# Graph attention in a 16-sequence block: graph values by transfers, zero rows from token sums, label products on GpSimd

## What is computed

```python
row_zero = v.sum(-1) == 0
q_exp = where(row_zero[..., None], 0.0, q[:, None, :])
self_feat = concatenate([v, q_exp], -1) @ W_self.T + b_self
output = self_feat; kv = self_feat[:, :20]
for d in range(2):
    A = (adj if d == 0 else swapaxes(adj, 1, 2))[:, :, :20, :]   # int32, 11 labels an edge
    cond = A.sum(-1); vb = A @ w_bias + b_bias
    aff = where(cond > 0, q_d . k_d / 4, NEG) + vb                # 16 heads of 16 channels
    output += softmax(aff) @ kv, through Wout[d], + bout[d]
x = v + relu(output)
```

## Time and profile before

| | |
|---|---|
| three runs | 832.12, 834.24, 836.28 us, median 834.24 |
| profiled execution | 834.01 us, its span 832.3 us |
| busy share of the span | PE 92%, DVE 59%, ACT 57%, POOL 45% |
| share of weight loads (PEld) | 68% |
| graph stage | from 27.8 us to about 270 us |
| mean granted clock of TensorE | 0.981 of full speed |

### The profile page before, as it was taken

The page is one execution under the profiler, slowest core; times in us unless marked ns, Lnnn a source line. Parts: engine busy times, 40 slices in busy tenths (PEclk is TensorE's granted clock), DMA queues, the critical chain, the costliest instruction groups (busy, mean ns, idle before and its releaser), DMA issues.

```text
span 832.3 us, 15511 instructions
## 1 busy us (share of the span) xinstructions
PE 767.1 (92%) x4964; PEld 561.9 (68%) x4964; DVE 489.9 (59%) x1030; ACT 477.3 (57%) x765; POOL 370.9 (45%) x612
## 2 busy tenths in 40 slices
PE   4989999999998489999999999999878999999997
PEld 3878778788875245666665556666545888888885
DVE  1378888888888745666665566655433443444433
ACT  1334444444444357777777777777655655555553
POOL 0157575757573455555555555554730212222110
PEclk9989999999999889999999999999989999999999
DMA  8701312121300666556665666566600000000001
GB/s 248 246 23 48 95 48 91 49 92 49 93 14 13 116 115 115 116 115 115 114 115 112 109 110 117 108 116 113 115 14 1 1 26 26 26 25 14 26 26 39
DMA packets 68860, 65.58 MB, mean 79 GB/s; under 512 B 11089, under 2 KB 68049, under 8 KB 68817
## 3 DMA queue, kind: packets, MB, share of 16 engines
q1 hardware_dynamic: 67488, 64.87, 34.4%
q10 hardware_dynamic: 1328, 0.16, 0.1%
HBM read 48.09 MB, written 16.78 MB: 78 GB/s over the span
## 4 chain that ended last, share of the span: by engine, by line
PE 47%; ACT 8%; issue 5%; DVE 4%; DMA 1%; POOL 1%; SPq 1%; ACTq 0%; POOLq 0%
PE ps L1599 10%; PE ps L1613 10%; PE ps L1489 5%; PE ps L1475 5%; ACT probsT L828 4%; PE ps L1527 3%; PE ps L1427 3%; PE ps L1419 2%; PE ps L1508 2%; ACT w_ada L857 2%; PE ps L1442 1%; ACT projT L849 1%; DVE qk L1074 1%; DMA parts_dram<-w_ada 1%; PE ps L1411 1%
## 5 line engine op out<-in xcount | busy, mean ns | idle before, releaser
L828 ACT ACTIVATE probsT<-ps 128x1024 f32<-128x1024 f32 x128 | 130.8, 1022 | 48.6 <-PE ps L1475 46.6
L1222 DVE TENSOR_TENSOR hidden_low<-hidden,hidden_high 128x512 fp32r<-128x512 f32 x64 | 46.6, 728 | 107.7 <-ACT hidden_high L940 59.7
L1126 DVE TENSOR_REDUCE neg_max<-ps 128x4 bf16<-128x344 f32 x128 | 64.2, 512 | 58.2 <-PE ps L1442 57.3
L1475 PE MATMUL ps<-q_stack,k_stack 97*128 97x256 bf16 x512 | 79.7, 279 | 9.0 <-ACT probsT L828 6.0
L1475 PEld LDWEIGHTS ps<-q_stack,k_stack 97*128 97x128 bf16 x512 | 43.4, 99 | 65.9 <-issue 30.6
L937 ACT ACTIVATE hidden<-ps,b_fc 128x512 f32<-128x512 f32 x64 | 44.1, 690 | 69.7 <-PE ps L1599 69.7
L1489 PE MATMUL ps<-probsT,v_ones 128*32 128x256 f32 x1024 | 69.3, 389 | 9.6 <-ACT probsT L828 9.5
L617 POOL TENSOR_TENSOR scores<-scores,row_max 128x640 f32<-128x640 f32 x32 | 40.8, 1275 | 76.7 <-DVE row_max L975 76.7
L1419 PE MATMUL ps<-w_qkv,x1T 128*128 128x512 f32 x128 | 63.7, 621 | 2.8 <-DVE rest L1133 2.8
L1325 PE MATMUL ps<-x_res,w_q 128*128 (+1 forms) x256 | 63.1, 391 | 0.0
L1325 PEld LDWEIGHTS ps<-x_res,w_q 128*128 128x128 f32 x256 | 46.9, 193 | 10.9 <-issue 5.5
(11 more groups left out here) (177 smaller groups left out, 1882.9 us busy)
## 6 DMA issues: line engine op xcount, KB each, us to landing
parts_dram<-w_ada SPq DMA_DIRECT2D x96, 128.0 KB
q_stack<-parts_dram SPq DMA_DIRECT2D x96, 128.0 KB, 3.9
k_stack<-parts_dram SPq DMA_DIRECT2D x32, 256.0 KB, 6.4
adj<-in_adj SPq DMA_DIRECT2D x16, 440.0 KB, 4.2
xT<-in_xT SPq DMA_DIRECT2D x16, 256.0 KB, 2.9
x_in<-in_x SPq DMA_DIRECT2D x16, 256.0 KB, 2.7
k_stack<-parts_dram SPq DMA_DIRECT2D x32, 128.0 KB, 5.4
out_x<-result SPq DMA_DIRECT2D x16, 256.0 KB, 2.1
```

The source lines that it names most:

```text
L828: nc.scalar.activation(probsT[:, s % 4, :], ps[:, COLS:COLS + 2, :].rearrange("p a n -> p (a n)"), ACT.Exp).then_inc(exp_made, 1)
L1126: nc.vector.tensor_reduce(places[:, :, k], ps[:, ROW_BANKS[n % 2], 0:4 * KP].rearrange("p (a g) -> p a g", a=4), AX_X, ALU.max, negate=Tru ...
L1222: nc.vector.tensor_tensor(hidden_parts[1][:, s % H_SLOTS, :], hidden[:, s % RAW, :], hidden_parts[0][:, s % H_SLOTS, :], ALU.subtract).the ...
L1475: mm = nc.tensor.matmul(ps[:, COLS + j, kt * N:(kt + 1) * N], k_stack[:, par, place, kt * P:(kt + 1) * P], q_stack[:, par, place, :], star ...
```

## The change

- **Values by transfers.** In setup, PE makes the values with tokens on the partitions (three tiles of 120, 120 and 80 rows by 512 channels), ACT copies them, SP stores them to a DRAM tensor v_dram. In each turn four transfers bring the values of b into v_blocks, whose other elements are zero since the setup. The masks on POOL, the value transposes on PE and the copy on ACT are gone; k_all goes through four banks.
- **Zero rows from token sums.** SP loads x of batch f + 1 with tokens on the partitions into x_res, ACT copies it with an accumulated sum of each row (row_totals), DVE makes of these a diagonal of ones and zeros in bf16 (nonzero, in the turn before), and PE multiplies it by ones: cond is made from PSUM. The row sums on PE and nz are gone.
- **Label products.** ACT copies the edges to floats behind cond, POOL multiplies these in place by the label weights, behind the second subtraction; DVE keeps the counts.
- Waits follow: among them, the raw scores of b wait for cond of f, the output transposes of c for the output of c - 1.

```diff
+V_BATCHES = 6
+V_TILES = (B + V_BATCHES - 1) // V_BATCHES
...
+        v_dram = nc.dram_tensor("v_dram", (B * M, 2 * F), F32, kind="Internal").ap()
...
+                K_BANKS = (4, 0, 1, 2)
+
+                def v_count(v):
+                    return min(V_BATCHES, B - v * V_BATCHES) * M
...
+                    for v in range(V_TILES):
+                        sp.wait_ge(v_rows_out, v + 1)
+                        sp.dma_start(v_dram[v * V_BATCHES * M:v * V_BATCHES * M + v_count(v), :], v_rows[0:v_count(v), v, :]
+                                     ).then_inc(v_stored, 16)
...
+                    for v in range(V_TILES):
+                        act.wait_ge(v_rows_mm, v + 1)
+                        nc.scalar.activation(v_rows[0:v_count(v), v, :], ps[0:v_count(v), 5 + v, :], ACT.Copy).then_inc(v_rows_out, 1)
                     for c in range(2 * C2):
-                        act.wait_ge(kv_mm, 2 * c + 1)
-                        nc.scalar.activation(k_all[:, c, :], ps[:, 4, 0:B * M], ACT.Identity,
+                        act.wait_ge(kv_mm, c + 1)
+                        nc.scalar.activation(k_all[:, c, :], ps[:, K_BANKS[c], 0:B * M], ACT.Identity,
                                              bias=b_k[:, c // C2, c % C2:c % C2 + 1]).then_inc(kv_out, 1)
-                        act.wait_ge(kv_mm, 2 * c + 2)
-                        nc.scalar.activation(v_all[:, c, :], ps[:, 5, 0:B * M], ACT.Copy).then_inc(kv_out, 1)
...
+                    nc.vector.memset(v_blocks[:], 0.0).then_inc(v_zeroed, 1)
...
+                    for v in range(V_TILES):
+                        for k in range(C2):
+                            mm = nc.tensor.matmul(ps[0:v_count(v), 5 + v, :], feat20[:, k, v * V_BATCHES * M:v * V_BATCHES * M + v_count(v)],
+                                                  w_o[:, :, k, :], start=(k == 0), stop=(k == C2 - 1))
+                        mm.then_inc(v_rows_mm, 1)
                     for c in range(2 * C2):
                         d, f = c // C2, c % C2
-                        for bank, w in ((4, w_k), (5, w_o)):
-                            ge(pe, kv_out, 2 * c + bank - 5)
-                            for k in range(C2):
-                                mm = nc.tensor.matmul(ps[:, bank, 0:B * M], w[:, d, k, f * P:(f + 1) * P], feat20[:, k, :],
-                                                      start=(k == 0), stop=(k == C2 - 1))
-                            mm.then_inc(kv_mm, 1)
+                        for k in range(C2):
+                            mm = nc.tensor.matmul(ps[:, K_BANKS[c], 0:B * M], w_k[:, d, k, f * P:(f + 1) * P], feat20[:, k, :],
+                                                  start=(k == 0), stop=(k == C2 - 1))
+                        mm.then_inc(kv_mm, 1)
...
+        def value_blocks(b, par):
+
+            ge(sp, mix_mm, b - 1)
+            rows = v_dram[bass.ds(b * M, M), :].rearrange("m (g h d) -> m g h d", g=H // 2, d=HD)
+            for h in range(4):
+                sp.dma_start(v_blocks[h * M:(h + 1) * M, par, :, h * HD:(h + 1) * HD], rows[:, :, h, :]).then_inc(v_in[par], 16)
+
+        x_by_batch = t["x"].rearrange("(b t p) f -> b p t f", b=B, p=P)
+
+        def x_tokens(f, par):
+
+            sp.dma_start(x_res[:, bass.ds(f * T, T), :], x_by_batch[bass.ds(f, 1)].rearrange("b p t f -> p (b t) f")
+                         ).then_inc(x_tokens_in[par], 16)
+
         def graph_turn(f, b, c, par):
-
             if f is not None and not (isinstance(f, int) and f == 0):
                 ge(sp, feat_mm, f - 1)
                 sp.dma_start(xT[:, par], t["xT"][:, bass.ds(f * N, N)].rearrange("(k p) n -> p k n", p=P)).then_inc(xT_in[par], 16)
-                ge(sp, lab_w, f - 1)
+                ge(sp, edges_float, f - 1)
                 ge(sp, cnt_made, f - 1)
+                ge(sp, diag_made, f)
                 sp.dma_start(adj[:, par].rearrange("p (t e) -> p t e", t=T),
                              t["adj"][bass.ds(f * N, N), :].rearrange("(t p) e -> p t e", p=P)).then_inc(adj_in[par], 16)
+            if isinstance(f, int) and f == 0:
+                x_tokens(0, 0)
+            if following(f) is not None:
+                x_tokens(following(f), 1 - par)
             if b is not None:
                 ge(sp, x_made, b - 1)
                 sp.dma_start(x_in[:, 1 - par], t["x"][bass.ds(b * N, N), :].rearrange("(t p) f -> p t f", p=P)
                              ).then_inc(x_arrived[1 - par], 16)
+                if isinstance(b, int) and b == 0:
+                    sp.wait_ge(g["v_stored"], 16 * V_TILES)
+                    sp.wait_ge(g["v_zeroed"], 1)
+                value_blocks(b, 1 - par)
...
+        def label_products(f):
+            pool.wait_ge(edges_float, f + 1)
+            edges = weighted[:].rearrange("p (e l) -> p e l", l=L)
+            nc.gpsimd.tensor_tensor(edges, edges, w_label[:].unsqueeze(1).broadcast_to([P, E2, L]), ALU.mult).then_inc(lab_w, 1)
...
             if f is not None:
-
-                ge(pool, vt_mm, 2 * f)
-                for k in range(2 * C2):
-                    nc.gpsimd.tensor_tensor(v_masked[:, k], v_all[:, k, bass.ds(f * M, M)].unsqueeze(1).broadcast_to([P, HT, M]),
-                                            own, ALU.mult).then_inc(vm_made, 1)
+                label_products(f)
...
+        def float_edges(f, par):
+            act.wait_ge(adj_in[par], loads(f, par))
+            ge(act, lab_made, f)
+            nc.scalar.activation(weighted[:], adj[:, par], ACT.Copy).then_inc(edges_float, 1)
...
-        def take_values(b, par):
-            act.wait_ge(vt_mm, 2 * b + 2)
-            ge(act, mix_mm, b - 1)
-            nc.scalar.activation(v_blocks[:, par], ps[0:G4, 0, :].rearrange("p (c v) -> p c v", v=64),
-                                 ACT.Copy).then_inc(vb_made, 1)
+        def row_totals(n, par):
+            act.wait_ge(x_tokens_in[par], loads(n, par))
+            ge(act, diag_made, n)
+            for tt in range(T):
+                nc.scalar.activation(summed[:, tt, :], x_res[:, bass.ds(n * T + tt, 1), :].rearrange("p a f -> p (a f)"), ACT.Copy,
+                                     accum_out=row_total[:, tt:tt + 1]).then_inc(totals_made, 1)
 
         def graph_turn(f, b, c, par):
+            if isinstance(f, int) and f == 0:
+                row_totals(0, 0)
             if f is not None:
 
-                act.wait_ge(nz_made, f + 1)
+                act.wait_ge(nz_mm, f + 1)
                 ge(act, feat_out, f)
                 for k in range(C2):
-                    nc.scalar.activation(cond[:, k, :], nz[:], ACT.Identity, bias=b_self[:, k:k + 1],
+                    nc.scalar.activation(cond[:, k, :], halves(ps, 4)[:, 0, :], ACT.Identity, bias=b_self[:, k:k + 1],
                                          scale=q_cond[:, k, bass.ds(f, 1)]).then_inc(cond_made, 1)
+                float_edges(f, par)
             if c is not None:
                 take_weights(c, 0)
                 take_weights(c, 1)
+            if following(f) is not None:
+                row_totals(following(f), 1 - par)
             if f is not None:
                 take_queries(f, par, 0)
             if b is not None:
                 exponentials(b, 1 - par, 0)
-                take_values(b, 1 - par)
                 exponentials(b, 1 - par, 1)
...
         def nonzero(f):
-
-            dve.wait_ge(sums_mm, f + 1)
-            ge(dve, cond_made, C2 * f)
-            nc.vector.tensor_scalar(nz[:], halves(ps, 4)[:, 0, :], 0.0, None, ALU.not_equal).then_inc(nz_made, 1)
+            dve.wait_ge(totals_made, T * (f + 1))
+            ge(dve, nz_mm, f)
+            nc.vector.scalar_tensor_tensor(out=nz_diag[:], in0=row_total[:].unsqueeze(2).broadcast_to([P, T, P]), scalar=0.0,
+                                           in1=ident_b[:].unsqueeze(1).broadcast_to([P, T, P]), op0=ALU.not_equal, op1=ALU.mult
+                                           ).then_inc(diag_made, 1)
 
         def features(f):
             dve.wait_ge(feat_mm, f + 1)
             dve.wait_ge(cond_made, C2 * (f + 1))
             nc.vector.tensor_tensor(feat_at(f), halves(ps, 1), cond[:], ALU.add).then_inc(feat_out, 1)
 
-        def label_products(f, par):
-
+        def edge_counts(f, par):
             dve.wait_ge(adj_in[par], loads(f, par))
-            edges = adj[:, par].rearrange("p (e l) -> p e l", l=L)
-            nc.vector.tensor_reduce(count[:], edges, AX_X, ALU.add).then_inc(cnt_made, 1)
-            nc.vector.tensor_tensor(weighted[:].rearrange("p (e l) -> p e l", l=L), edges,
-                                    w_label[:].unsqueeze(1).broadcast_to([P, E2, L]), ALU.mult).then_inc(lab_w, 1)
+            nc.vector.tensor_reduce(count[:], adj[:, par].rearrange("p (e l) -> p e l", l=L), AX_X, ALU.add).then_inc(cnt_made, 1)
...
         def graph_turn(f, b, c, par):
+            if isinstance(f, int) and f == 0:
+                nonzero(0)
             if f is not None:
-                nonzero(f)
```

(49 more changed lines are left out.)

48 lines of the change are left out of this document (25 added, 23 removed).

## The result

The changed kernel takes 845.12 us (median of 4, 839.76 to 847.50) where the kernel before took 834.30 in the same comparison: ratio 1.0131, 95% interval [1.0097, 1.0164], slower. The forecast was 836.0 in 821 to 845. The profiled execution has a span of 845.4 us, 13.1 more than before's 832.3. It is the longest of the four: its mean granted clock is 0.966, that of the others is 0.972, 0.973 and, in the one of 839.76 us, 0.981, where the kernel before has 0.977 to 0.985 in all 63 executions that ran beside the experiments. The medians are 10.8 us apart, so the 13.1 taken apart here are a little more than the usual execution has. The two tables of windows, cut at the same events (start of the graph stage, start of the third turn, start of the last, its end at the last raw scores, first `rest` on DVE), say where.

What follows compares the result with a forecast made beforehand. It took a loop over PE, DVE and POOL, 13.76 us a turn, as the bound. Start +4.7, graph turns -0.5, layernorm turn -1.0, last turn -1.4 gave +1.8 on 834.2: 836 us, range 821 to 845.

Steps and rivals of the forecast that it cites:

- PE alone could turn in 12.0: Steady graph turn: PE's own work and wait shrink by 1.85 us, so PE alone could turn in 12.0 us.
- They alternate, and the one that waited goes first: DVE with two SBUF inputs and POOL: one stands still until the other's instruction ends, then the waiting one goes.
- The turn stays at 13.8: Graph stage: a loop over the engines sums to 13.76 us a turn, gaining 0.5 us in place of 22.
- Rivals B: Graph turn: no_edge (L999) does not wait for the normalising; turn 13.1 us, kernel 828 us; chance 0.18.
- C: Graph turn: DVE's diagonal does not collide with POOL at all; turn 12.4 us, kernel 819 us; chance 0.12.
- I take 1.68, as 640 is the nearest size: POOL's label product: 880 elements at 1.70 ns each take 1.68 us, bounds 1.07 and 2.5.
- rival D: POOL's label product exceeds 1.68 us, its rows being short; every 0.1 us costs 1.3 us in all; chance 0.20.
- +4.7: Start: longer setup and late tokens put the first queries at 37.8 for 33.08 us; bounds +2.5 and +6.5.
- the 4.4 from there to the queries stay: Start: from the features' start at 33.4 us to the first queries at 37.8 remains 4.4 us.
- Behind it, DVE orders the transition as now: Transition behind the last graph turn: DVE sets its order as before, so no time was added.
- ACT "hidden": ACT's added copy and sums run hidden; if not, 0.9 us before the weight copies returns as PE's wait.
- A: The loop over the engines as counted, kernel 836 us, give or take 4; chance 0.50.

Runs made afterwards that it cites:

- number 5: Changed kernel with label products back on DVE, DVE diagonal moved ahead of the second scores, and tokens of batches 0 and 1 loaded in setup: 811.65 us.
- number 6: Changed kernel with POOL's label product cut from one instruction of 880 elements into two of 440: 832.05 us.
- number 12: Changed kernel with 8 products that nobody reads put on PE ahead of the first nonzero rows: 837.54 us.
- numbers 2: Changed kernel with the tokens of batches 0 and 1 loaded in setup, ahead of the late weights: 838.01 us.
- number 3: Changed kernel with the DVE diagonal moved ahead of the second scores and tokens of batches 0 and 1 loaded in setup: 820.49 us.
- number 1: Changed kernel with the DVE diagonal moved behind the edge counts, ahead of the second scores: 828.55 us.
- numbers 9: Changed kernel with 16 products that nobody reads put on PE ahead of the first nonzero rows: 841.58 us.
- number 8: Kernel before with only the label products moved: float copy on ACT, product on POOL behind the second shift: 867.19 us.

## Why the prediction was wrong, point by point

- **"PE alone could turn in 12.0":** right; number 5 turns in 12.06. (1.85 less in 13 turns is 24 us; the 25 is a slip.)
- **"They alternate, and the one that waited goes first":** right, and it carries the case. The diagonal ends 0.27 behind the label product (0.29 forecast), `no_edge` behind the normalising; number 6 shows that whole instructions exclude each other. That is the rule cited from the Trainium skill (SBUF — State Buffer, "Who interferes with whom"), and the trace agrees, with 1325 against 415 ns. By the page's rule alone one would not know who goes next; the rows say that.
- **"The turn stays at 13.8":** right in kind. The loop was counted as 13.76; with the label product at 1.92 in place of 1.68 it is 14.0, and eleven turns took 13.95. Rivals B (13.1) and C (12.4) are out.
- **"I take 1.68, as 640 is the nearest size":** wrong, mis-sized by 0.24 in each turn. By rival D's own rule that is 3.1 us, 839, already slower by over 0.5%. Measured, the loop cost less than that: the eleven plain turns came out 2.0 us over their forecast, and the layernorm turn 0.8 under. The line through 160 and 640 elements did not hold for the label product's 880 in rows of 11. Number 6 gives a second size in rows of 11, 440 elements in 1.05 us (median): from there to 880 it is 2.0 ns an element, where the rows of 160 and 640 gave 1.70. The cost per element was higher, as rival D had it. That the short rows are the reason was not tested by itself.
- **The start, "+4.7":** this is the step that failed, with the transition below: +9.0 measured. Its first half came out: the stage began 1.8 later (1.1 forecast) and the features at 33.88 (33.4). Then "the 4.4 from there to the queries stay" failed: it took 6.1 us, because the features ran at the lower level behind PE's 4.95 us without work (the modulations then took 3.00 for 2.75), and the queries themselves took 5.39 for 3.70. That makes +8.5 at the end of turn 0. Turn 1 gave back 1.3 and turn 2, partly at the lower level, took 1.8, where the sum had nothing for either. The text had the fall of the clock only in its upper bound, +6.5, and priced it too low. Number 12 shows the clock's part best: products that nobody needs, put into that wait, take 3.3 us off what follows it. The features' half of that goes with the long wait; the queries' half also falls behind a wait of 2.48 in numbers 2 and 5 and not in 3, and why is open. Part of the +1.8 need not be an effect of the change, as the end of the same setup moves by up to 1.9 us between executions (28.19 in number 1, 30.08 in number 12).
- **"Behind it, DVE orders the transition as now":** wrong by 4.25 us. About 0.6 of it is there at full clock (23.97 for 23.34), the rest is the mix, transposes and squares at the lower level. That the granted clock costs it is shown by numbers 9 and 12. Why it falls in some executions there and not in others is open: the two have the same waits in front (1.51, 0.58, 0.36 or 0.37, 2.13 or 2.14 and 1.11 us).
- **"Queues nothing", ACT "hidden":** right here. No wait for `v_blocks` or for the tokens shows in a steady turn, with DMA share up from 0.23 to 0.31. In number 8 it isn't hidden: PE waits 1.41 us for the weight copy behind it where the kernel before waits 0.46, which is the 0.9 named there.
- **Layernorm turn and last turn:** -1.0 and -1.4 forecast, -1.8 and -1.1 measured.
- **The chances:** A was the likeliest and its loop is what happened, but A's "give or take 4" held only the loop's errors. The start's upper bound and D together give 836 + 1.8 + 3.1 = 841, and the transition had no range at all. That 845.12 lies just above the range's 845 says little for the sum: +1.8 was forecast and 10.8 measured.

**How much the clock costs in the usual execution.** The mean granted clock of every execution is on record, the stretches only of the profiled ones. Number 12's profiled execution took 844.24 us at 0.971, its eleven others 835.26 to 838.88 at 0.979 to 0.985. So the clock was at full speed for longer in the eleven, which fits a transition and a turn 2 at full clock (3.5 and 2.8 us in the rows above), but a mean doesn't say in which stretch. In the same way the changed kernel took 845.03 and 845.20 us at 0.973 and 0.972, and 839.76 in its one execution at 0.981, where the kernel before averages 834.2 in six executions at that clock. So about half of the 10.8 us between the medians is there at equal mean clock, as far as one execution can tell, and the other half goes with a clock that is lower more of the time than the kernel before ever had it (0.977 at least).

The gain of 24 us that the removed PE work held out is real: number 3 has half of it (12.6 below the kernel before) by moving one DVE instruction and two transfers, number 5 nearly all (22.2), with the label products back on DVE.

## What to carry to other kernels

When a change puts a VectorE instruction with two SBUF inputs near a long GpSimd one, look at which instructions are side by side, not at the engines' sums: order, and length of the single instruction, were worth 13 to 17 us here, while the engines' sums had promised a gain. Put such an instruction where GpSimd is idle, and split long GpSimd instructions so that others get in. And price a new gap on TensorE twice: its own length, and what the products behind it cost at the lower clock (1.5 us for the features here, only behind gaps of 4.95 and more; 1.7 for the queries, also behind 2.48 in two kernels of three). Read the mean granted clock of all executions, not of the profiled one alone.

## What was not expected

- Splitting POOL's label product adds POOL work (1.92 us to twice 1.05) and takes 13.1 us off the kernel.
- `no_edge` costs 138 or 1264 ns by what stands ahead of it. It reads one tensor and a number, so the exclusion is not limited to instructions with two tensor inputs. (The same section of the Trainium skill states that a `tensor_scalar` can enter a mode that takes the shared pair. The 1264 against 138 ns fit that; no row here names the mode.)
- A sum kept by ACT is a second instruction:

```profile
138.60 0.40 ACT L825 ACTIVATE summed<-x_res 128x256 bf16 x1
138.91 0.19 ACT L825 ACTIVATION_READ_ACCUMULATOR summed<-x_res 128x1 f32 x1
```

- The clock fell in the kernel before too, in a turn in which PE never waited (3.03 us for 1.89).
- The clock can stay up or fall in the same stretch of the same instructions from one execution to another, worth 3.5 us, and a single profile shows only one of the two.
